# Second cross attention of a two-layer transformer kernel: where in a slot TensorE turns the probabilities

## The chip, the cores and the metric

The kernel runs on one core of a Trainium2 chip. A core has TensorE (PE, matrix products; PEld is its loading of weights), VectorE (DVE), ScalarE (ACT), GpSimd (POOL) and SyncE (SP, which here only issues transfers). The engines run side by side, each through its own list of instructions in order, and wait for each other by semaphores. TensorE has two clock levels, 1.2 and 2.4 GHz; the profile gives the granted clock as a share of the full one. The metric is the device time of one execution in microseconds (us), less is better.

## The reference

Two layers stand one after the other on x (4 x 1024 rows of 256). Each is self attention, cross attention on a context of 77 rows, and a gated feed-forward. The change touches the cross attention of the second layer alone (16 heads of 64):

```python
h = layer_norm(hidden_states, norm2_g, norm2_b)
q = (h @ wq).reshape(b, n, H, HD).transpose(0, 2, 1, 3)       # H, HD = 16, 64
k = (kv_in @ wk).reshape(b, l, H, HD).transpose(0, 2, 1, 3)   # l = 77
v = (kv_in @ wv).reshape(b, l, H, HD).transpose(0, 2, 1, 3)
probs = jax.nn.softmax(einsum('bhnd,bhld->bhnl', q, k) * HD ** -0.5, axis=-1)
out = einsum('bhnl,bhld->bhnd', probs, v).transpose(0, 2, 1, 3).reshape(b, n, H * HD)
hidden_states = out @ wo + bo + hidden_states
```

## The kernel before

The stage is the function `cross_block` (L2597), here with `narrow` false. The 4096 rows are cut into eight tiles of 512, and the 16 heads into eight pairs. One tile and one pair make a **slot**; there are 64 slots, n = 8t + p. For a slot p stands for its place in the tile, 0 to 7. The keys and values of the context were made in an earlier stage. Float32 precision is held by splitting each operand into a high and a low part and adding three products (hi x hi, lo x hi, hi x lo).

Every engine runs the same loop over n with its own part of the work, and parts of different slots stand in the body of one n. TensorE's body in the kernel before is, in this order:

- `score(n)` (L2998 on): 24 matmuls of 64 rows against 78 columns into the score bank `s` (matmuls on L3020). It waits until DVE has emptied `s`.
- `query(n + 2)` (L2986 on, matmuls on L2994): six matmuls, the query of the slot after next. None for n of 62 and more.
- `values(n - 3)` (L3037 on, L3046): two float32 matmuls, which the trace shows as four. It waits for `t_done`: ScalarE's copy of the turned probabilities of slot n - 3.
- `project(...)` (L3050 on, L3062): 24 matmuls of the output projection, in the slots with p = 7, 0, 3 and 4 only.
- `flip(n - 2)` (L3024 on, L3034): eight transposes of the probabilities into the one turned bank `t`. It waits for `t_done`, here that ScalarE has copied the bank of slot n - 3 out, and for `p_norm`, that GpSimd has divided the probabilities of slot n - 2 by their sums.
- `turn(...)` (L2977 on, L2983): eight transposes of normalised rows for a tile to come, in the slot with p = 5 of the first six tiles.

ScalarE's body in slot n is the exponential of slot n (L2951), the high part of the query (`f_q_hi`, L2931), the high part of the output of slot n - 3 (`f_o_hi`, L2938), in the slot with p = 6 of the first six tiles four instructions that scale the turned rows (`f_ht` L2915, `f_h_hi` L2920), and last the copy of the turned bank of slot n - 2 (`f_probs_t`, L2966). ScalarE can't do one of them ahead of the one listed before it.

DVE's body is the maximum of the scores (`f_mx`, L2878), their difference (L2882), sums and reciprocals of the slot before (as the loop numbers them), in slots behind a project the addition to x, the low parts of query (`f_q_lo`, L2851) and output (`f_o_lo`, L2857), in the slot with p = 1 of the first six tiles the statistics of rows (L557 to L569), and normalised rows in p = 4. GpSimd divides (L2812).

Query, output, projection and turned rows share four banks `r0` to `r3`, handed out in the order of the program; `clear(u)` waits until the fourth unit back has been emptied. The change leaves this order of units as it was.

Of the kernel before, what the change touches and what calls it, by code (L numbers as in the profile page):

```python
# [96 lines left out]
class Program:  # L97
# [2499 lines left out]
    def cross_block(self, L, x_sb, ident, g, b, wq, wo, bo):  # L2597
# [5 lines left out]
        SLOTS = TILES * PAIRS  # L2603
# [17 lines left out]
        def q_of(n):  # L2621
            if narrow:
                t = (n - 1) // PAIRS + 1
                return [(t, c) for c in range(QCH)] if n % PAIRS == 1 and 0 < t < TILES else []
            return [divmod(n + 2, PAIRS)] if 0 <= n < SLOTS - 2 else []

        def acc_of(n):
            if not 0 <= n < SLOTS:
                return None
            if narrow:  # L2630
                return (n // PAIRS, n % PAIRS // 2) if n % 2 else None
            return divmod(n, PAIRS)

        def y_of(n):
            for part, first in ((0, 7), (1, 11)):
                t, j = divmod(n - first, PAIRS)
                if 0 <= t < TILES and j < 2:
                    return (t, part, j)
            return None

        def turn_of(n):
            t, p = divmod(n - TURN_AT, PAIRS)
            return t + LEAD if p == 0 and 0 < t + LEAD < TILES else None
# [19 lines left out]
        with ExitStack() as st:  # L2663
# [305 lines left out]
            def _(pe):  # L2969
# [7 lines left out]
                def turn(t):  # L2977
                    pe.wait_ge(n_["chain"], (t + 1) * self.STATS_STEPS)
                    for c in range(DC):
                        u = at["tp", t, c]  # L2980
                        clear(u)
                        for j in range(TB):
                            ins = t_.transpose(bank[u % 4][:, j * P:(j + 1) * P], xhat[:, j, c * P:(c + 1) * P], ident[:, :])  # L2983
                        ins.then_inc(r_ready, 1)

                def query(t, c):  # L2986
                    u = at["q", t, c]
                    pe.wait_ge(hh_done, DC * (t + 1))
                    if not narrow:
                        pe.wait_ge(hl_done, t + 1)  # L2990
                    clear(u)
                    passes = [(k, 0, 0) for k in range(DC)] if narrow else self.H_PASSES
                    for j, (k, a, bb) in enumerate(passes):
                        ins = t_.matmul(bank[u % 4][:, :], wqr[a][:, k, c * P:(c + 1) * P], h[bb][t % 2][:, k, :],  # L2994
                                        start=j == 0, stop=j == len(passes) - 1)
                    ins.then_inc(r_ready, 1)

                def score(n):  # L2998
                    t, p = divmod(n, PAIRS)
                    bt = t // 2  # L3000
                    if p == 0 and t % 2 == 0:
                        pe.wait_ge(kv_in[bt % KVB], KV * (bt // KVB + 1))
                    if n > 0:
                        pe.wait_ge(s_free, n)
                    if narrow:
                        if p == 0:
                            pe.wait_ge(moved, 96 * (t + 1))
                        passes = [(qs[t % 2], p, kt[bt % KVB][0])]
                        rows = 3 * HD
                    else:  # L3010
                        pe.wait_ge(q_lo, n + 1)
                        q0, q1 = qn
                        k0, k1 = kt[bt % KVB]
                        passes = [(q0, n % 4, k0), (q0, n % 4, k1), (q1, n % 4, k0)]
                        rows = HD
                    for qb in range(TB):
                        for x, (q, slot, k) in enumerate(passes):
                            for r in range(2):
                                part = slice(64 * r, 64 * r + rows)
                                ins = t_.matmul(sbk[:, r, qb * MP:(qb + 1) * MP], q[part, slot, qb * P:(qb + 1) * P], k[part, p, :],  # L3020
                                                start=x == 0, stop=x == len(passes) - 1, tile_position=(64 * r, 0))
                    ins.then_inc(s_ready, 1)

                def flip(n):  # L3024
                    if n > 0:
                        pe.wait_ge(t_done, n)
                    if narrow:
                        busy = kt[0][0][:, :, :].rearrange("p j m -> p (j m)")
                        for r in range(2):
                            t_.matmul(tbk[:, r, :], busy[:, 0:P], busy[:, 0:512], start=True, stop=True)  # L3030
                    pe.wait_ge(p_norm, n + 1)
                    for r in range(2):
                        for qb in range(TB):
                            ins = t_.transpose(tbk[0:M, r, qb * P:(qb + 1) * P], pr[:, n % PR, r, qb, :], ident[:, :])  # L3034
                    ins.then_inc(t_ready, 1)

                def values(n):  # L3037
                    t, c = acc_of(n)
                    bt, u = t // 2, at["acc", t, c]
                    pe.wait_ge(t_done, n + 1)  # L3040
                    clear(u)
                    pairs = (n - 1, n) if narrow else (n,)
                    for x, m in enumerate(pairs):
                        for r in range(2):
                            row = W * (2 * x + r)
                            ins = t_.matmul(bank[u % 4][row:row + W, :], vs[bt % KVB][:, m % PAIRS * 2 + r, :], pt[:, m % 2, r, :],  # L3046
                                            start=True, stop=True, tile_position=(0, row))
                    ins.then_inc(r_ready, 1)

                def project(t, part, j):  # L3050
                    u, half = at["y", t, part, j], OCH // 2
                    pe.wait_ge(kind_sem["acc"], nth("acc", t, part * half + half - 1))
                    if narrow:
                        pe.wait_ge(wo_in, WOL)
                    else:
                        pe.wait_ge(w_lo, 2)
                    clear(u)
                    for k in range(2):
                        tok = slice((2 * j + k) * P, (2 * j + k + 1) * P)
                        work = [(c, x, w) for c in range(part * half, part * half + half) for x, w in (((0, 0),) if narrow else ((0, 0), (0, 1), (1, 0)))]  # L3060
                        for i, (c, x, w) in enumerate(work):
                            ins = t_.matmul(bank[u % 4][:, k * D:(k + 1) * D], o[x][:, c, tok], wor[w][:, c, :],  # L3062
                                            start=i == 0, stop=i == len(work) - 1)
                    ins.then_inc(r_ready, 1)
# [9 lines left out]
                for n in range(FIRST, LAST):  # L3074
                    if 0 <= n < SLOTS:
                        score(n)
                    for key in q_of(n):
                        query(*key)
                    if acc_of(n - 3):
                        values(n - 3)  # L3080
                    if y_of(n):
                        project(*y_of(n))
                    if 0 <= n - 2 < SLOTS:
                        flip(n - 2)
                    if turn_of(n - 1):
                        turn(turn_of(n - 1))

# [341 lines left out]
```

## Time and profile before

| | us |
|---|---|
| median of three runs | 4222.43 |
| lowest and highest of them | 4221.16 and 4227.47 |
| the profiled execution | 4226.14 |
| its span, first to last instruction | 4224.3 |
| this stage's slots in it, about | 3475.7 to 3916.2 |

In the timeline rows the first number is the start of a group of instructions in us from the span's start, the second its duration, then come engine, line, operation, output<-input by the program's names, shapes, and how many instructions the row joins; in square brackets stands the idle time of the engine ahead of it and who ended it. Matmuls are pipelined, so one starts before the one ahead has ended: what a part costs TensorE is read from start to start.

### The profile page before, as it was taken

How to read it: one execution, taken by the hardware profiler on the slowest of the kernel's cores; microseconds unless marked ns; L12 is line 12 of the kernel's file. 1: busy time of each engine (PE TensorE's matmuls, PEld its weight loads, DVE VectorE, ACT ScalarE, POOL GpSimd, SP SyncE). 2: the span in 40 equal slices, each digit the busy share in tenths (PEclk: the TensorE clock that was granted, in tenths of full speed). 3: DMA queues.
4: the chain of work that ended last, by engine and by line, in shares of the span. 5: the costliest groups of instructions: out<-in, count | busy, mean ns of one | idle time of the engine just before them, and what ended most of it. 6: DMA issues, size and time to landing. Idle time of an engine off the chain costs nothing. (4 is left out here: it accounts for less than half of the span.)

```text
span 4224.3 us, 64439 instructions
## 1 busy us (share of the span) xinstructions
PE 3916.2 (93%) x24639; PEld 2597.8 (61%) x24639; DVE 2766.8 (65%) x4547; ACT 1839.8 (44%) x2746; POOL 1859.1 (44%) x1203
## 2 busy tenths in 40 slices
PE   3799999995898997998999999999999979999899
PEld 2543443433456886885666666666666647777787
DVE  6599999953446654435767666676767637665665
ACT  1367777771453333442333333333333324444333
POOL 1288970001113102004777877877787753222200
PEclk9789999986779998997999999999999989999999
DMA  4734434405631105883211121111112010000100
GB/s 158 181 56 75 60 57 46 45 1 79 106 54 49 25 13 177 305 308 123 73 54 51 51 76 51 51 57 70 51 51 73 29 31 10 10 10 1 42 14 17
DMA packets 314325, 294.96 MB, mean 70 GB/s; under 512 B 133324, under 2 KB 237196, under 8 KB 313764
## 3 DMA queue, kind: packets, MB, share of 16 engines
q1 hardware_dynamic: 311364, 281.88, 25.8%
q0 software_dynamic: 2656, 8.97, 0.7%
q8 instruction: 197, 3.23, 0.3%
q14 instruction: 108, 0.88, 0.1%
HBM read 161.92 MB, written 127.28 MB: 68 GB/s over the span
## 5 line engine op out<-in xcount | busy, mean ns | idle before, releaser
L1741 POOL TENSOR_TENSOR f_sums<-f_sums,f_probs 128x1024 f32<-128x1024 f32 x384 | 915.5, 2384 | 154.6 <-ACT f_probs L1860 116.9
L1860 ACT ACTIVATE f_probs<-f_st 128x1024 f32<-128x1024 f32 x512 | 525.0, 1027 | 938.6 <-PE f_st L1906 933.9
L1758 DVE TENSOR_REDUCE f_mx<-f_s 128x1 f32<-128x512 f32 x1024 | 659.8, 686 | 381.0 <-PE f_s L1883 369.6
L1369 DVE TENSOR_REDUCE f_mx<-f_s 128x1 f32<-128x512 f32 x1024 | 638.7, 683 | 53.2 <-PE f_s L1501 31.2
L1481 ACT ACTIVATE f_probs<-f_st 128x512 f32<-128x512 f32 x1024 | 536.1, 600 | 234.1 <-PE f_st L1518 233.8
L1883 PE MATMUL f_s<-f_k,f_q 64*128 64x512 f32 x3072 | 514.7, 414 | 19.1 <-DMA f_k<-k 12.9
L1906 PE MATMUL f_st<-f_q,f_k 64*128 64x512 f32 x3072 | 486.0, 390 | 1.1 <-ACT f_probs L1860 1.0
L1920 PE MATMUL f_acc<-f_probs,f_v 128*64 128x512 f32 x2048 | 466.1, 597 | 0.0
L1883 PEld LDWEIGHTS f_s<-f_k,f_q 64*128 64x128 f32 x3072 | 341.4, 189 | 166.8 <-issue 112.5
L1906 PEld LDWEIGHTS f_st<-f_q,f_k 64*128 64x128 f32 x3072 | 367.0, 185 | 25.8 <-ACT f_probs L1860 3.8
L1518 PE MATMUL f_st<-f_q,f_k 50*128 50x512 f32 x1024 | 336.1, 480 | 6.6 <-ACT f_probs L1481 6.4
L588 POOL TENSOR_TENSOR f_ve<-f_var,f_const 128x4 f32<-128x4 f32 x48 | 10.0, 209 | 698.4 <-DVE f_var L569 698.2
L1518 PEld LDWEIGHTS f_st<-f_q,f_k 50*128 50x128 f32 x1024 | 137.5, 188 | 283.7 <-ACT f_probs L1481 262.6
L1920 PEld LDWEIGHTS f_acc<-f_probs,f_v 128*64 128x64 f32 x2048 | 141.5, 137 | 266.1 <-issue 257.2
L1501 PE MATMUL f_s<-f_k,f_q 48*128 48x512 f32 x1024 | 267.9, 457 | 22.8 <-DMA f_k<-k 22.5
L1530 PE MATMUL f_acc<-f_probs,f_v 128*32 128x512 f32 x2048 | 279.3, 619 | 0.0
L1781 DVE RECIPROCAL f_rd<-f_s 128x512 f32<-128x512 f32 x64 | 214.9, 3358 | 71.7 <-PE f_s L1929 71.7
L1906 PE MATMUL f_st<-f_m,f_mones 64*128 64x512 f32 x1024 | 248.4, 390 | 0.0
L3281 ACT ACTIVATE f_gate<-f_pg,f_bias 128x512 f32<-128x512 f32 x128 | 88.0, 688 | 348.8 <-PE f_pg L3327 348.8
L765 DVE TENSOR_TENSOR f_stage<-f_pc,f_stage 128x512 f32<-128x512 f32 x160 | 110.3, 691 | 190.2 <-ACT f_stage L795 190.1
L1737 POOL TENSOR_TENSOR f_sums<-f_probs 128x1024 f32<-128x1024 f32 x64 | 153.2, 2394 | 184.0 <-ACT f_probs L1860 184.0
L3206 DVE SCALAR_TENSOR_TENSOR f_u<-f_pa,f_bias,f_gate 128x512 f32<-128x512 f32 x128 | 96.1, 751 | 201.4 <-PE f_pa L3327 195.7
(320 smaller groups left out, 7861.8 us busy)
## 6 DMA issues: line engine op xcount, KB each, us to landing
q<-f_stage SPq DMA_DIRECT2D x80, 512.0 KB, 2.9
k<-f_stage SPq DMA_DIRECT2D x80, 512.0 KB, 2.8
f_q<-q SPq DMA_DIRECT2D x32, 1024.0 KB, 5.1
f_k<-k SPq DMA_DIRECT2D x32, 1024.0 KB, 7.5
v<-f_v_stage SPq DMA_DIRECT2D x64, 256.0 KB, 3.1
f_v<-v SPq DMA_DIRECT2D x32, 512.0 KB, 8.7
f_q<-q SPq DMA_DIRECT2D x96, 128.0 KB, 4.3
f_k<-k SPq DMA_DIRECT2D x96, 128.0 KB, 7.1
```

What stands on the lines that cost most here:

```text
L1369: v.tensor_reduce(mx[:, i % 2, c:c + 1], bank[u % 4][:, :], AX_X, ALU.max).then_inc(s_free, 1)
L1481: a_.activation(probs[:, n % NP, e % 2, :], stb[k % 3][:, :], ACT.Exp, scale=L.scale).then_inc(p_ready, 1)
L1501: t.matmul(bank[u % 4][:, :], q[cur][rows, j, qb * P:(qb + 1) * P], k_[cur][rows, j, f * HALF:(f + 1) * HALF], start=True, stop=True, tile ...
L1518: t.matmul(stb[n % 3][:, :], k_[cur][rows, j, c * P:(c + 1) * P], q[cur][rows, j, half * HALF:(half + 1) * HALF], start=True, stop=True, t ...
L1530: ins = t.matmul(acc[W * h:W * h + W, :], vs[cur][:, c, h, :], p, start=c == 0, stop=c == KC - 1, tile_position=(0, W * h))
L1741: g_.tensor_tensor(out, out, probs[:, n % NP, :, :], ALU.add).then_inc(sum_done, 1)
L1758: v.tensor_reduce(mx[:, i % 2, c:c + 1], bank[u % 3][:, :], AX_X, ALU.max).then_inc(s_free, 1)
L1781: v.reciprocal(rd[:, half, :], bank[u % 3][:, :]).then_inc(s_free, 1)
L1860: a_.activation(probs[:, s % NP, :, :], stb[s % 2][:, :, :], ACT.Exp, scale=L.scale).then_inc(p_ready, 1)
L1883: ins = t.matmul(bank[u % 3][:, :], q[cur][rows, a, qb * P:(qb + 1) * P], k_[cur][rows, c, f * HALF:(f + 1) * HALF], start=r == 0, stop=r ...
L1906: ins = t.matmul(stb[s % 2][:, h, :], lhs, rhs, start=r == 0, stop=r == 3, tile_position=(64 * h, 0))
L1920: ins = t.matmul(acc[W * h:W * h + W, :], vs[cur][:, c, h, :], probs[:, s % NP, h, :], start=c == 0, stop=c == KC - 1, tile_position=(0, W ...
```

## The change

TensorE's call of `flip(n - 2)` moves from behind `project` to directly behind `score(n)`, ahead of `query`, `values` and `project`. No instruction is added or removed, and the lists of the other four engines are the same.

```diff
                 for n in range(FIRST, LAST):
                     if 0 <= n < SLOTS:
                         score(n)
+                    if 0 <= n - 2 < SLOTS:
+                        flip(n - 2)
                     for key in q_of(n):
                         query(*key)
                     if acc_of(n - 3):
                         values(n - 3)
                     if y_of(n):
                         project(*y_of(n))
-                    if 0 <= n - 2 < SLOTS:
-                        flip(n - 2)
                     if turn_of(n - 1):
                         turn(turn_of(n - 1))
```

TensorE in the kernel before, slot 30 (tile 3, p = 6), from the last matmuls of its scores to the first of the next slot's:

```order
L3020 MATMUL f_s<-f_k_hi,f_q_lo 128x78 x2
L2994 MATMUL f_r<-f_h_hi,f_wq_hi 128x512
L2994 MATMUL f_r<-f_h_lo,f_wq_hi 128x512
L2994 MATMUL f_r<-f_h_hi,f_wq_lo 128x512
L2994 MATMUL f_r<-f_h_hi,f_wq_hi 128x512
L2994 MATMUL f_r<-f_h_lo,f_wq_hi 128x512
L2994 MATMUL f_r<-f_h_hi,f_wq_lo 128x512
L3046 MATMUL f_r<-f_probs_t,f_v 64x512 x2
L3034 MATMUL f_t<-ident,f_probs 77x128 x8
L3020 MATMUL f_s<-f_k_hi,f_q_hi 128x78 x2
```

The eight transposes (L3034) stand last, with the values (L3046) ahead of them. The same stretch of TensorE in the changed kernel:

```order
L3020 MATMUL f_s<-f_k_hi,f_q_lo 128x78 x2
L3034 MATMUL f_t<-ident,f_probs 77x128 x8
L2994 MATMUL f_r<-f_h_hi,f_wq_hi 128x512
L2994 MATMUL f_r<-f_h_lo,f_wq_hi 128x512
L2994 MATMUL f_r<-f_h_hi,f_wq_lo 128x512
L2994 MATMUL f_r<-f_h_hi,f_wq_hi 128x512
L2994 MATMUL f_r<-f_h_lo,f_wq_hi 128x512
L2994 MATMUL f_r<-f_h_hi,f_wq_lo 128x512
L3046 MATMUL f_r<-f_probs_t,f_v 64x512 x2
L3020 MATMUL f_s<-f_k_hi,f_q_hi 128x78 x2
```

The transposes moved ahead of the query and the values; between the values and the next transposes only the next scores are left.

ScalarE in the same slot 30, word for word the same in both kernels:

```order
L2951 ACTIVATE f_probs<-f_probs 128x616
L2931 ACTIVATE f_q_hi<-f_r 128x512
L2938 ACTIVATE f_o_hi<-f_r 128x512
L2915 ACTIVATE f_ht<-f_r,f_b,f_g 128x512 x2
L2920 ACTIVATE f_h_hi<-f_r,f_b,f_g 128x512 x2
L2966 ACTIVATE f_probs_t<-f_t 77x1024
L2951 ACTIVATE f_probs<-f_probs 128x616
```

Nothing moved here: the copy of the turned bank (L2966) still stands behind the output's high part (L2938), which reads what the values wrote.

## Rows read from the trace of the kernel before

**Rows 1.** The page's first line: span and instructions.
```profile
span 4224.3 us, 64439 instructions
```
**Rows 2.** Stretches: length, busy PE, PEld, DVE, ACT, POOL, clock, DMA share, GB/s.
```profile
3490.00:3900.00 410.00, 404.05 (x3329) 306.57 (x3330) 277.83 (x487) 183.64 (x271) 114.19 (x116) 0.99 0.04 8
3475.00:3493.00 18.00, 17.77 (x97) 14.40 (x96) 10.89 (x23) 6.04 (x10) 1.22 (x1) 0.50 0.00 1
3514.00:3517.00 3.00, 3.00 (x8) 1.72 (x9) 2.56 (x5) 1.37 (x3) 2.46 (x2) 0.50 0.00 0
```
**Rows 3.** Waits of 3490 to 3900: who for whom, us in total, times, longest.
```profile
POOL f_probs L2812 <- DVE f_rden L2890: 290.9, 62, 7.3
```
**Rows 4.** Timeline of TensorE, slot 25 (p = 1) and the start of slot 26.
```profile
3641.89 0.30 PE L3020 MATMUL f_s<-f_k_hi,f_q_hi 64*128 64x78 f32 x2
...
3643.35 0.50 PE L2994 MATMUL f_r<-f_h_hi,f_wq_hi 128*128 128x512 f32 x1
...
3644.94 1.08 PE L3046 MATMUL f_r<-f_probs_t,f_v 77*64 77x512 f32 x4
3645.95 1.10 PE L3034 MATMUL f_t<-ident,f_probs 128*77 128x128 f32 x8
3646.98 0.30 PE L3020 MATMUL f_s<-f_k_hi,f_q_hi 64*128 64x78 f32 x2
```
**Rows 5.** Timeline of ScalarE, slot 30 (p = 6), and one row of slot 31.
```profile
3678.23 0.59 ACT L2938 ACTIVATE f_o_hi<-f_r 128x512 fp32r<-128x512 f32 x1
3678.71 1.45 ACT L2915 ACTIVATE f_ht<-f_r,f_b,f_g 128x512 f32<-128x512 f32 x2
...
3681.36 1.03 ACT L2966 ACTIVATE f_probs_t<-f_t 77x1024 f32<-77x1024 f32 x1
...
3683.66 0.60 ACT L2938 ACTIVATE f_o_hi<-f_r 128x512 fp32r<-128x512 f32 x1 [0.19 <-PE f_r L3046]
```
**Rows 6.** Timeline of TensorE, slot 31 (p = 7).
```profile
3678.99 0.30 PE L3020 MATMUL f_s<-f_k_hi,f_q_hi 64*128 64x78 f32 x2
...
3680.97 0.47 PE L2994 MATMUL f_r<-f_h_hi,f_wq_hi 128*128 128x512 f32 x1 [0.46 <-ACT f_h_hi L2920]
...
3682.54 1.08 PE L3046 MATMUL f_r<-f_probs_t,f_v 77*64 77x512 f32 x4
```
**Rows 7.** Timeline of TensorE and ScalarE in the last slots, 63 and 64.
```profile
3890.82 1.08 PE L3046 MATMUL f_r<-f_probs_t,f_v 77*64 77x512 f32 x4 [0.37 <-ACT f_probs_t L2966]
...
3894.77 1.03 PE L3034 MATMUL f_t<-ident,f_probs 128*77 128x128 f32 x8
...
3895.84 1.02 ACT L2966 ACTIVATE f_probs_t<-f_t 77x1024 f32<-77x1024 f32 x1 [2.47 <-PE f_t L3034]
...
3896.91 1.08 PE L3046 MATMUL f_r<-f_probs_t,f_v 77*64 77x512 f32 x4 [1.11 <-ACT f_probs_t L2966]
```
**Rows 8.** Timeline of VectorE: slots 25 and 26, and the low output of slot 31.
```profile
3647.11 0.68 DVE L2857 TENSOR_TENSOR f_o_lo<-f_r,f_o_hi 128x512 fp32r<-128x512 f32 x1
...
3649.84 0.79 DVE L2878 TENSOR_REDUCE f_mx<-f_s 128x8 f32<-128x616 f32 x1
...
3684.30 0.69 DVE L2857 TENSOR_TENSOR f_o_lo<-f_r,f_o_hi 128x512 fp32r<-128x512 f32 x1
```
**Rows 9.** Timeline of ScalarE, slot 26 (p = 2).
```profile
3651.50 0.72 ACT L2951 ACTIVATE f_probs<-f_probs 128x616 f32<-128x616 f32 x1 [3.40 <-DVE f_probs L2882]
...
3653.08 1.02 ACT L2966 ACTIVATE f_probs_t<-f_t 77x1024 f32<-77x1024 f32 x1
```
**Rows 10.** Timeline of TensorE, slots 5 and 6 of the first tile.
```profile
3510.10 1.09 PE L2983 MATMUL f_r<-ident,f_xhat 128*128 128x128 f32 x8 [0.88 <-DVE f_xhat L2836]
...
3513.70 0.70 PE L2994 MATMUL f_r<-f_h_hi,f_wq_hi 128*128 128x512 f32 x1 [0.52 <-DVE f_q_lo L2851]
...
3516.46 1.42 PE L3046 MATMUL f_r<-f_probs_t,f_v 77*64 77x512 f32 x4
...
3517.80 1.10 PE L3034 MATMUL f_t<-ident,f_probs 128*77 128x128 f32 x8
```

## The prediction

> **What bounds the kernel now.** The change acts in one stage of the span [rows 1], so I read that stage first by stretches: in the 410 us from 3490 to 3900 TensorE is busy for 404.05, DVE for 277.83, ScalarE for 183.64, and the granted clock is 0.99 of the upper level, 2.4 GHz [rows 2]. TensorE bounds the stage, and each us in which it waits is a us of the kernel. The timeline of one slot gives the price of each part, from start to start [rows 4]: scores 1.46 us, query 1.59, values 1.01, flip 1.03, together 5.09. All parts follow each other without a wait. A project adds 2.94: in the last slots the flip starts 3.95 behind the values, whose own 1.01 goes off [rows 7].
>
> So the question is whether the flip finds its inputs ready at its new place. It has two. GpSimd's division is far ahead: GpSimd itself waited 290.9 us of the 410 for work, 4.7 a slot [rows 3], and the flip of a slot comes two slots behind its scores; moving it up by 2.60 us (query and values) leaves this input in time. The other is the copy of slot n - 3 by ScalarE, which must have emptied the bank. That one is the heart.
>
> **The chain behind the wait.** ScalarE does the copy behind the high part of the output, and that reads what TensorE's values wrote in the same slot. This order stands in both kernels. Let V be the start of the values in a slot. The output's high part starts 1.12 behind V when it has to wait for the values (3682.54 to 3683.66) [rows 5, 6]. What follows it starts 0.48 later (3678.23 to 3678.71) [rows 5]. The copy lasts 1.02, and TensorE goes on 0.05 behind its end (3895.84 + 1.02 = 3896.86, then 3896.91) [rows 7]. So the next flip can start at V + 1.12 + 0.48 + 1.02 + 0.05 = **V + 2.67**. Where does TensorE want it? Before: query of the next slot and its values stood between, so V + 1.01 + 1.03 + 1.46 + 1.59 + 1.01 = V + 6.10, and nothing waited. Now: values 1.01, scores 1.46, and then the flip, at **V + 2.47**. Query and values of the next slot are queued behind it.
>
> **The sum, place by place.**
>
> (a) Plain slots. The wait is 2.67 - 2.47 = 0.20. It falls only where no project and no turn stands between the values and the next flip, since a project covers 2.94 and a turn, eight transposes like the flip, about 1.03. Projects are in p = 7, 0, 3, 4, so the flips of p = 0, 1, 4, 5 are covered; p = 6 is covered by the turn of p = 5 in the first six tiles. What is left: p = 2 in seven tiles (in the first there is no copy yet), p = 3, 6 and 7 in tiles 6 and 7 only, which is 13 flips with p = 3 elsewhere counted in (b). 13 x 0.20 = **+2.6 us**.
>
> (b) p = 3 in tiles 1 to 5. In p = 1 DVE runs the statistics behind the low part of the output. That low part starts 0.64 behind the high part (3683.66 to 3684.30) [rows 5, 8], so at V + 1.12 + 0.64 = V + 1.76, V in p = 1; before, it came 0.6 us sooner in the slot. The maximum of p = 2 starts 2.73 behind it (3647.11 to 3649.84) [rows 8], at V + 4.49; the exponential 1.66 behind that (3649.84 to 3651.50) [rows 8, 9], the copy 1.58 behind the exponential (3651.50 to 3653.08) [rows 9]: V + 7.73, and it frees TensorE at V + 8.80. TensorE wants the flip of p = 3 at V + 1.01 + 1.46 + 0.20 + 1.03 + 1.59 + 1.01 + 1.46 = V + 7.76. Wait 1.04, five times: **+5.2 us**.
>
> (c) p = 7 in the first six tiles. In p = 6 ScalarE runs four scalings between output and copy; the copy starts 2.65 behind them (3678.71 to 3681.36) [rows 5]. The flip of p = 7 is free at V + 1.12 + 0.48 + 2.65 + 1.03 + 0.05 = V + 5.33 instead of the wanted V + 2.47: wait 2.86. Before, the query of p = 7 already waited for the same scalings: 3680.97 - 3678.99 - 1.46 = 0.52 [rows 6]. That one ends before the new one does, and goes. Net 2.34, six times: **+14.0 us**.
>
> (d) The end. With no scores left, the values of slots 60 to 63 waited for the copy of their own probabilities: 0.43 once (the row's bracket has 0.37) and 1.11 three times [rows 7], 3.8 in all. With the flip ahead, projects cover three of these copies, and only the last is bare: the values of 62 stand behind the flip of 63 and its copy behind their output, V + 2.67 against V + 1.01, 1.66. Net **-2.1 us**.
>
> (e) The clock. In the first tile TensorE waited three times within 4 us (0.88 and 0.52 in the rows shown), and then ran at 0.50, which is 1.2 GHz, from 3514 to 3517 [rows 2, 10]. There query and values cost 4.10 us (3513.70 to 3517.80) instead of 1.59 + 1.01 = 2.60: 1.5 us. A wait of 2.86 with transposes behind it, as in (c), is nearest to this row, so I take one such fall for each: 6 x 1.5 = **+9.0 us**. Bounds: nothing, since TensorE waited 1.11 twice near the end, with 6 us between, and its clock held; and twice as much, if the fall lasts through a second such stretch.
>
> (f) The beginning. From 3475 to 3493 the clock stands at 0.50 though TensorE is busy [rows 2]; it rises behind that, in slot 2. Now the first flip comes ahead of the query of slot 2. If the rise comes later by one stretch like the 3 us at 0.50 in (e), that is half of it, **+1.5 us**; bounds 0 and +5.
>
> (g) The new neighbours (values to scores, scores to flip, flip to query). No row shows them. The nearest is the change from scores to query, where the last pair of scores takes about 0.1 us more than those inside. I take 0, as one such neighbour goes for each that comes, with 0.1 x 64 = 6.4 us to either side.
>
> Sum: 2.6 + 5.2 + 14.0 - 2.1 + 9.0 + 1.5 = **+30.2 us**. On the profiled execution's 4226.1 that is 4256.3; the median of the runs is 3.7 lower, so I predict 4252.6, say **4253 us**.
>
> **Rivals.** *The clock holds* (e and f at 0): +19.7, 4242. For it speaks that it held at 1.11 twice; against it, that the new wait is two and a half times as long. *The clock falls for longer*, also at the start: +9 to +18 more, 4262 to 4271. *The waits are absorbed.* For it: TensorE's weight loading is busy only 306.57 of 410 us, 75% [rows 2], so it might catch up. Then only (d) is left, about 4220, within 0.2%. Against it: scores, query, values and flip start in fixed steps, and a step that starts late has no shorter form behind it. The Trainium skill (Perfetto Trace Analysis, Identifying the Most-Contended Engine) says that matmul busy time is no good measure of how near TensorE is to its limit and that weight loading is to be read instead; by it the stage would have a quarter of its time free, and this rival would be the forecast. No run here shows yet which holds; the fixed steps in the trace speak against it. *Faster.* If the copy of the bank were done by V + 2.47, no flip would wait. Then the 0.52 of (c) is gone six times (3.1), the end gives 3.8 less 1.7, and if (g) falls well, 6.4: 11.6 less, 4211. It turns on 0.20 us in the plain slots, but on 2.86 in (c), where the four scalings can't move; so it is nearly shut. That the change does nothing is ruled out by the order of the instructions.
>
> **How the numbers follow.** Forecast with falls of the clock 0.50; clock holds 0.25; clock falls longer 0.10; absorbed 0.11; faster 0.04. The likeliest has its own range of 4246 to 4260 with (g). The range for 8 in 10 takes in the clock that holds, with (g) at its low end, 4242 - 6.4 = 4236, and about half of the longer falls, 4268. A measurement tells about 0.2%, 8.4 us, from no change. Faster by more 0.04, within it 0.11, slower 0.85.
>
> **What would show it.** In the waits of the changed kernel TensorE's flip (L3034) should wait for ScalarE's copy (L2966): about 25 to 27 us in all, the longest near 2.9 in p = 7 of the first six tiles, near 1.0 in p = 3 of tiles 1 to 5, and 0.2 elsewhere. The query's wait for `f_h_hi` should be gone, and of the waits of the values for copies one near 1.7 be left. The granted clock should dip behind each wait of (c). DVE, ScalarE and GpSimd keep their busy time. The prediction is wrong if the flips wait but the stage isn't longer (absorbed), if the flips in p = 7 wait under 2 us (chain misread), or if slots without any wait have another length than 5.09 (neighbours).

## The result and the profile after

The changed kernel took 4252.97 us, median of five runs (4246.03 to 4258.73), against 4221.16 us, median of five runs of the kernel before (4217.26 to 4227.47). The ratio is 1.0075, 95% interval 1.0063 to 1.0088: 0.75% slower. The prediction was 4253, range 4236 to 4268.

That the sum meets the median to the last digit is luck in part: the term for the plain slots was 4.9 us too high, the terms for p = 3 and for the first tile together 4.6 us too low, and one statement of the prediction was false. So the profile is read term by term below.

The page's first line, as [rows 1]:

```profile
span 4251.2 us, 64439 instructions
```

The stage again runs on TensorE, and now it waits. The stretch that answers to the first of [rows 2], same columns:

```profile
3490.00:3900.00 410.00, 381.55 (x3068) 292.20 (x3068) 261.09 (x449) 176.68 (x255) 104.62 (x110) 0.95 0.04 8
```

TensorE's busy time in the 410 us fell from 404.05 to 381.55, and the mean clock from 0.99 to 0.95. From the first score to the last project the stage took 462.8 us (3471.49 to 3934.30) instead of 433.0 (3475.69 to 3908.72): **+29.8 us**. The rest of the span was 2.9 us shorter in this execution; nothing in it was changed.

Who makes TensorE wait, in the waits of the stage (3475 to 3945; who for whom, us in total, times, longest):

```profile
PEld f_t L3034 <- ACT f_probs_t L2966: 31.4, 28, 2.9
...
PE f_t L3034 <- ACT f_probs_t L2966: 25.8, 13, 2.8
...
PE f_t L3034 <- POOL f_probs L2812: 0.3, 1, 0.3
```

The flips wait for ScalarE's copy, in all 25.8 us, the longest 2.8. These are the 13 waits that the timeline marks: six of 2.81 in p = 7, five of 1.09 in p = 3 of tiles 1 to 5, and in tile 0 one of 2.41 and one of 1.09. The waits of 0.2 of the plain slots aren't in this total; they are read from the starts of the flips. The query's wait for `f_h_hi` is gone from the list. The timeline of tile 1 between p = 6 and p = 7 shows the chain link by link, the counterpart of [rows 5, 6] (TensorE and ScalarE, in order of time):

```profile
3576.91 1.08 PE L3046 MATMUL f_r<-f_probs_t,f_v 77*64 77x512 f32 x4
...
3577.92 0.31 PE L3020 MATMUL f_s<-f_k_hi,f_q_hi 64*128 64x78 f32 x2
...
3578.04 0.60 ACT L2938 ACTIVATE f_o_hi<-f_r 128x512 fp32r<-128x512 f32 x1 [0.42 <-PE f_r L3046]
...
3578.53 1.44 ACT L2915 ACTIVATE f_ht<-f_r,f_b,f_g 128x512 f32<-128x512 f32 x2
...
3581.18 1.03 ACT L2966 ACTIVATE f_probs_t<-f_t 77x1024 f32<-77x1024 f32 x1
...
3582.26 1.99 PE L3034 MATMUL f_t<-ident,f_probs 128*77 128x128 f32 x8 [2.81 <-ACT f_probs_t L2966]
```

The rows belong to slots 14 and 15. With V = 3576.91 the flip starts at V + 5.35, and the scores stand 1.46 wide from V + 1.01, so it was wanted at V + 2.47: 2.88 later, of which the row marks 2.81 as idle time. Here is also the clock: this flip's eight transposes take 1.64 us to the next query instead of 0.86, and the 3 us from its start on stand at half clock:

```profile
3582.00:3585.00 3.00, 2.74 (x11) 2.55 (x12) 0.07 (x1) 0.81 (x2) 1.22 (x1) 0.50 0.00 0
```

A plain slot, counterpart of [rows 4], slot 14 (p = 6), where no flip waits. It takes 4.90 us instead of 5.09: the flip costs 0.86 (3574.48 to 3575.34) ahead of the query, where it cost 1.03 ahead of the scores.

```profile
3573.02 0.30 PE L3020 MATMUL f_s<-f_k_hi,f_q_hi 64*128 64x78 f32 x2
3574.48 1.10 PE L3034 MATMUL f_t<-ident,f_probs 128*77 128x128 f32 x8
3575.34 0.48 PE L2994 MATMUL f_r<-f_h_hi,f_wq_hi 128*128 128x512 f32 x1
3576.91 1.08 PE L3046 MATMUL f_r<-f_probs_t,f_v 77*64 77x512 f32 x4
3577.92 0.31 PE L3020 MATMUL f_s<-f_k_hi,f_q_hi 64*128 64x78 f32 x2
```

And p = 3 in tile 3 (slot 27), counterpart of [rows 8, 9]. DVE's low output and the maximum behind the statistics, GpSimd's division, ScalarE's copy, and TensorE's flip:

```profile
3661.30 0.69 DVE L2857 TENSOR_TENSOR f_o_lo<-f_r,f_o_hi 128x512 fp32r<-128x512 f32 x1 [0.33 <-ACT f_o_hi L2938]
...
3664.04 0.79 DVE L2878 TENSOR_REDUCE f_mx<-f_s 128x8 f32<-128x616 f32 x1
...
3666.68 1.22 POOL L2812 TENSOR_TENSOR f_probs<-f_probs,f_rden 128x616 f32<-128x616 f32 x1 [5.58 <-DVE f_rden L2890]
...
3667.27 1.01 ACT L2966 ACTIVATE f_probs_t<-f_t 77x1024 f32<-77x1024 f32 x1
...
3668.34 1.10 PE L3034 MATMUL f_t<-ident,f_probs 128*77 128x128 f32 x8 [1.09 <-ACT f_probs_t L2966]
```

The copy ends at 3668.28 and lets the flip go. But GpSimd's division ends at 3667.90, only 0.38 earlier, while the flip was wanted at 3667.18 (its scores start at 3665.72 and are 1.46 wide). The prediction had called this input far ahead.

### The profile page after: what moved, and what is told of

It reads as the page before. It is cut to its first block and busy times, and to the rows that moved or that the text cites. A ratio compares the mean times of both kernels' runs of the same rounds, so it can differ in the third digit from the quotient of the medians.

```text
span 4251.2 us, 64439 instructions
## 1 busy us (share of the span) xinstructions
PE 3918.8 (92%) x24639; PEld 2604.7 (61%) x24639; DVE 2773.8 (65%) x4547; ACT 1844.6 (43%) x2746; POOL 1858.8 (44%) x1203
## 5 line engine op out<-in xcount | busy, mean ns | idle before, releaser
L1883 PE MATMUL f_s<-f_k,f_q 64*128 64x512 f32 x3072 | 515.4, 414 | 18.4 <-DMA f_k<-k 12.2
L1501 PE MATMUL f_s<-f_k,f_q 48*128 48x512 f32 x1024 | 268.1, 457 | 19.8 <-DMA f_k<-k 19.5
```

The source lines that it names most:

```text
L1501: t.matmul(bank[u % 4][:, :], q[cur][rows, j, qb * P:(qb + 1) * P], k_[cur][rows, j, f * HALF:(f + 1) * HALF], start=True, stop=True, tile ...
L1883: ins = t.matmul(bank[u % 3][:, :], q[cur][rows, a, qb * P:(qb + 1) * P], k_[cur][rows, c, f * HALF:(f + 1) * HALF], start=r == 0, stop=r ...
```

## Experiments

Slot lengths from one start of scores to the next, in us, each from the one profiled execution of its kernel, for tiles 1 to 5. The last column is the stage, from the start of the first scores to the start of the last project. The ratios below are against runs of the kernel before made together with each set of experiments (medians 4219.6 to 4220.4).

| kernel | p = 1 | p = 2 | p = 3 | p = 7 | last scores to last project | stage |
|---|---|---|---|---|---|---|
| before | 5.09 | 5.09 | 7.87 to 7.97 | 8.38 to 8.47 | 19.79 | 433.0 |
| changed | 4.90 | 5.17 | 9.01 to 9.09, once 10.52 | 12.10 to 12.36 | 17.88 | 462.8 |
| copy first | 4.90 | 5.16 | 8.76, once 10.26 | 8.46 | 19.58 | 438.3 |
| flip behind query | 4.93 | 5.16 | 7.88 to 7.96 | 9.3 to 9.4, or 10.6 | 17.78 | 437.3 |
| extra matmuls | 4.90 | 5.15 | 9.10 or 10.6 | 7.93 (p = 6: 7.85) | 17.77 | 457.1 |
| copy ahead of scaling | 4.90 | 5.16 | 10.5 to 10.6 | 10.8 to 10.9 | 17.87 | 458.1 |
| statistics in p = 0 | 4.90 | 5.11 | 8.06 | 13.3 to 13.4 | 17.87 | 460.7 |
| copy first and statistics | 4.90 | 4.90 | 7.85 to 7.93 | 8.38 to 8.47 | 16.39 | 424.7 |
| early where covered | 4.90 | 5.16 | 7.88 | 9.34, 10.7 or 13.6 | 18.81 | 446.1 |
| early in p = 7 only | 5.09 | 5.09 | 7.88 to 7.97 | 11.1 to 11.4, once 12.64 | 19.62 | 452.9 |
| statistics alone | 5.09 | 5.09 | 7.88 | 8.39 to 8.47 | 19.61 | 432.2 |

The whole kernel scatters by 10 to 37 us between executions, of the kernel before too (4206.61 to 4236.95 in one set), so a ratio tells a few tenths of a per cent, and the slots tell the mechanism: where the clock doesn't fall they repeat to 0.1 us from tile to tile. A stage length is of one execution, and how often the clock falls in others wasn't seen.

### Copy first

```diff
 (ScalarE, slot n)
+                    (copy of the turned bank of slot n - 2)
                     if 0 <= n < SLOTS:
                         act.wait_ge(s_free, n + 1)
                         a_.activation(flat, flat, ACT.Exp, ...)
...
-                    (copy of the turned bank of slot n - 2)
```

> The changed order on TensorE, and ScalarE's copy of the turned bank moved from the end of its slot to its front, ahead of the exponential. If the changed kernel is slower because the copy stands behind the output's high part (and the scaling) on ScalarE, all waits of the flips for the copy go: plain slots 4.90 us, p = 7 back to about 8.3 (its query then waits some 0.4 for the scaling), the last values wait under 0.3; the whole 9 us below the kernel before, near 4212. If it is slower because query and values stand later in their slot (late low parts of query and output on VectorE), nothing of that changes and it stays near 4250.

4221.0 us, ratio 1.0006 (0.9991 to 1.0021). With the flip in its new place and only the copy moved, the 0.75% are gone. All waits for the copy went, and p = 7 is back at 8.46. So nearly all of the price is where the prediction put it: the copy's place on ScalarE's list. In p = 7 the late query and values are no price. But the expected gain of 9 us didn't come, and in the profiled execution the stage is still 5.3 us longer than before. Waits of the stage (3475 to 3935) and two rows of slot 27:

```profile
PE f_t L3034 <- POOL f_probs L2812: 5.6, 8, 0.8
...
PE f_r L2994 <- ACT f_h_hi L2920: 1.8, 6, 0.3
```

```profile
3655.96 1.22 POOL L2812 TENSOR_TENSOR f_probs<-f_probs,f_rden 128x616 f32<-128x616 f32 x1 [5.59 <-DVE f_rden L2890]
...
3657.32 1.07 PE L3034 MATMUL f_t<-ident,f_probs 128*77 128x128 f32 x8 [0.79 <-POOL f_probs L2812]
```

The second input shows behind the first: in p = 3 the flip now waits 0.79 us for GpSimd's division, which ends at 3657.18, and the scores 0.19 for DVE. The slot keeps 0.88 of its 1.2 us, and in one of the five tiles the clock fell behind this wait of 0.79 (p = 3 at 10.26). The scores' wait for DVE is also why p = 2 stays at 5.16 here in tiles 1 to 5, while it is 4.91 and 4.90 in tiles 6 and 7, which have no statistics.

### Flip behind the query

```diff
                         score(n)
-                    if 0 <= n - 2 < SLOTS:
-                        flip(n - 2)
                     for key in q_of(n):
                         query(*key)
+                    if 0 <= n - 2 < SLOTS:
+                        flip(n - 2)
```

> Flip between query and values. If the price is the 2.67 us from values to the emptied bank, plain slots and p = 3 are free of waits, since the query's 1.6 us lies between, and p = 7 keeps a wait of about 0.75: some 4 us for it and 2 us less at the end, 4217 to 4226, no measurable difference from the kernel before, and no fall of the clock in p = 7. If any flip ahead of the values costs, it comes out well above 4230.

4225.1 us, ratio 1.0009 (0.9998 to 1.0021). The time is in the expected range, its make-up isn't as expected. In p = 7 the flip doesn't wait; the query ahead of it waits for the scaling, 1.3 us and not 0.5, since no flip stands any more between the values of p = 6 and the query. Waits of the stage:

```profile
PE f_r L2994 <- ACT f_h_hi L2920: 8.0, 6, 1.3
```

After this wait of 1.3 us the clock held in three of six tiles (p = 7 at 9.3 to 9.4) and fell in three (10.6), which was not expected.

### Extra matmuls against the fall of the clock

```diff
 (score(n), ahead of its matmuls)
+                    if turn_of(n - 3) and n > 0:
+                        fill = kt[bt % KVB][0][:, :, :].rearrange("p j m -> p (j m)")
+                        for k in range(12):
+                            t_.matmul(sbk[:, k % 2, :], fill[:, 0:P], fill[:, 0:512], start=True, stop=True)
```

> The changed kernel with twelve extra matmuls (128 x 512, some 2.6 us) ahead of the scores in p = 7 of the first six tiles; the scores overwrite what they write. They end within the 2.8 us that the flip waits anyway. If the 1.2 GHz stretch behind that wait costs, it goes and the kernel is about 6 x 1.3 = 8 us faster than the changed one, near 4244, with p = 7 slots of about 10.9 us instead of 12.2. If the clock plays no part, p = 7 stays at 12.2 or grows.

4249.2 us, ratio 1.0069 (1.0050 to 1.0088), so by the whole nothing can be told from the changed kernel. By the slots it can. The extra matmuls take 2.94 us in the length of p = 6, and p = 7 is 7.93; together 15.8 against 17.0 to 17.3 in the changed kernel, 1.2 to 1.5 less, with more work done. In the timeline (slots 14 and 15) the flip follows the scores without a wait and takes 0.86 us, that is at full clock:

```profile
3572.96 3.01 PE L3019 MATMUL f_s<-f_k_hi 128*128 128x512 f32 x12
3575.90 0.30 PE L3024 MATMUL f_s<-f_k_hi,f_q_hi 64*128 64x78 f32 x2
...
3577.36 1.10 PE L3038 MATMUL f_t<-ident,f_probs 128*77 128x128 f32 x8
...
3578.22 0.48 PE L2994 MATMUL f_r<-f_h_hi,f_wq_hi 128*128 128x512 f32 x1
```

So the fall is real and costs 1.2 to 1.5 us each time in tiles 1 to 5. The stage is 5.7 us shorter and not 8, mainly because the clock now fell in p = 3 of three tiles (10.6 instead of 9.1), where it had fallen once.

### The copy ahead of the scaling

```diff
 (ScalarE, slot n)
-                    if turn_of(n - 2):
-                        scale(turn_of(n - 2))
                     (copy of the turned bank of slot n - 2)
+                    if turn_of(n - 2):
+                        scale(turn_of(n - 2))
```

> The changed kernel with the four scalings of p = 6 behind the copy instead of ahead of it. The flip of p = 7 should wait 0.2 instead of 2.8, its query then 1.2 for the scaling, and the clock should hold there: p = 7 at about 9.2 us instead of 12.2, six times, 18 us less than the changed kernel, near 4235. Waits of p = 2 and p = 3 stay. If p = 7 is long for another reason, it stays at 12.

4237.6 us, ratio 1.0039 (1.0023 to 1.0055); half of the loss is back in the median. That is near the expected 4235, but not by the expected way: p = 7 came to 10.85 and not 9.2 in tiles 1 to 5, and the stage of the profiled execution, the slowest of the six, is only 4.7 us shorter than in the changed kernel. Why the median is 15 us lower isn't shown. The wait of the flip is gone and the query's for the scaling is there as expected, but the clock falls behind that one too, and behind the 1.09 in p = 3 in all five tiles. Both in the timeline, of tile 2 and of tile 3:

```profile
3634.18 0.62 PE L2994 MATMUL f_r<-f_h_hi,f_wq_hi 128*128 128x512 f32 x1 [0.99 <-ACT f_h_hi L2920]
...
3661.93 1.99 PE L3034 MATMUL f_t<-ident,f_probs 128*77 128x128 f32 x8 [1.09 <-ACT f_probs_t L2964]
```

The same wait of 1.09 with transposes of 1.99 us here, and of 1.10 us in slot 27 of the changed kernel: a wait of this size alone doesn't settle whether the clock falls.

### Statistics in p = 0

```diff
 (VectorE, slot n; the loops start one slot earlier)
-                    if turn_of(n + 3):
-                        self.norm_stats(dve, n_, x_sb, turn_of(n + 3))
+                    if turn_of(n + 4):
+                        self.norm_stats(dve, n_, x_sb, turn_of(n + 4))
```

> The changed kernel with VectorE's statistics in the slots with p = 0 instead of p = 1. If they make p = 3 long (9.1 us against 7.9 before), p = 3 of tiles 1 to 5 comes to about 8.05, like tiles 6 and 7 where there are none, and the stage is about 5 us shorter, 6.5 if the fall of the clock in tile 1 goes too: near 4247. If something else holds the flip of p = 3, it stays at 9.1.

4243.9 us, ratio 1.0054 (1.0027 to 1.0081). p = 3 came to 8.06 in tiles 1 to 5, as expected: the statistics made some 1.0 of the 1.2 us there. The stage is only 2.1 us shorter, since in p = 7 of tiles 1 to 5 the clock now stays at 1.2 GHz for about 6.8 us instead of 3.4 (13.4 instead of 12.2). The stretches of 1 us show 0.50 from 3687 to 3693 in tile 3, where the changed kernel has 3698 to 3701.

### Copy first and statistics in p = 0 together

The diffs of copy first and of the statistics, both applied to the changed kernel.

> Both repairs together: ScalarE's copy at the front of its slot and VectorE's statistics in p = 0. With the copy first alone, the flip of p = 3 still waited 0.79 us for GpSimd's division and the scores 0.2 for VectorE. If both come from the statistics, no wait is left in p = 3 (7.85 us) and p = 2 (4.90), and tiles 1 to 5 take 0.6 us less each than in the kernel before: stage near 430 us against 433.0, total near 4217. If GpSimd is late for another reason, p = 3 stays at 8.7.

4215.8 us, ratio 0.9991 (0.9976 to 1.0006): by the whole, no difference from the kernel before. Stage 424.7. No flip of the tiles behind the first waits for the copy, and one 0.6 us for GpSimd (3540 to 3920):

```profile
PE f_r L2994 <- ACT f_h_hi L2920: 1.5, 5, 0.3
...
PE f_t L3034 <- POOL f_probs L2812: 0.6, 1, 0.6
```

The same kernel, run again:

> The kernel with both repairs once more, with more rounds: its stage took 424.7 us against 433.0 in the kernel before, 8.3 less, 0.2% of the whole. If that is a gain of the kernel and not of one execution, the stage is 423 to 427 again and the ratio stays below 1, about 0.998; if the one execution was lucky, the stage comes out near 430 and the ratio at 1.

4215.4 us, ratio **0.9976 (0.9955 to 0.9996)**, stage 424.2. Of the two sets only this one puts the whole kernel's gain over the kernel before clear of nothing, and barely. The stage is shorter by 8.3 and 8.8 us, with the same slots in tiles 1 to 7 to 0.1 us; against the changed kernel the version is 38 us of stage shorter. Its counterpart is the kernel before with the diff of the statistics alone, the flip in its old place:

> The kernel before with VectorE's statistics in p = 0 and nothing else: the flip in its old place. If the gain of the repaired kernel comes from the early flip (0.2 us less in p = 1, 2 and 6, and a shorter end), this one shows none of it: all slots of tiles 1 to 7 as in the kernel before, 5.09 in p = 1, 2 and 6, stage 432 to 434. If the statistics alone bring it, its stage is as short as 425.

4223.1 us, ratio 1.0012 (0.9994 to 1.0031), stage 432.2, and slots as in the kernel before. So the statistics alone bring no gain: it comes with the early flip once nothing holds it, 0.19 us each in p = 1, 2 and 6, and with a shorter end (16.39 instead of 19.61). What of the end is due to the flip and what to the copy's new place wasn't separated; the kernel before with the copy first wasn't run.

### Early only where something covers it

```diff
+                    early = n % PAIRS in (0, 1, 4, 5) or (n % PAIRS == 6 and turn_of(n - 2)) or n >= SLOTS
+                    if early and 0 <= n - 2 < SLOTS:
+                        flip(n - 2)
...
+                    if not early and 0 <= n - 2 < SLOTS:
+                        flip(n - 2)
```

> The flip early only where a project or a turn stands ahead of it (p = 0, 1, 4, 5, and 6 of the first six tiles) and at the end; late as before in the others. By the chain from values to the emptied bank no flip waits: p = 1 and 6 at 4.90, p = 2 at 5.09, p = 3 at 7.9, p = 7 at 8.45, the end 1.9 us shorter, no dips of the clock in tiles 1 to 7: stage 428 to 430 us, total near 4217. If an early flip costs whatever stands ahead of it, it is slower than before.

4238.7 us, ratio 1.0043 (1.0024 to 1.0063): a miss. Behind tile 0 the flips do nearly as the chain says: from 3540 to 3920 one of them waits, 1.1 us, at the end. But p = 7 is 9.34, 10.7 or 13.6 instead of 8.45. With the flip of p = 6 moved ahead, its 1.03 us no longer stand between the values and the next query, and that waits for the scaling:

```profile
PE f_r L2994 <- ACT f_h_hi L2920: 6.7, 5, 1.3
```

Five waits of 1.3 us: behind one no fall of the clock (9.34), behind two a short one (10.7), and behind two one of some 10 us (13.6; the stretches of 1 us show 0.50 from 3631 to 3640). (p = 2 came to 5.16 and not 5.09.) The late flip had been the cover of another wait.

### Early in p = 7 only

```diff
+                    early = n % PAIRS == 7 and turn_of(n - 3)
```

> The flip early only in p = 7 of the first six tiles. The values of p = 6 then have the late flip behind them, so the early one is wanted at V + 3.50 and free at V + 5.33: wait 1.83, less the 0.5 that the query no longer waits, 1.3 us each, and 2.8 where the clock falls: 8 to 17 us in all, 4230 to 4239. Other slots as in the kernel before. If the wait in p = 7 isn't the copy behind the scalings, p = 7 stays near 8.4.

4240.1 us, ratio 1.0043 (1.0023 to 1.0063). In tiles 1 to 5 five waits of 1.9 us, as expected, p = 7 at 11.1 to 11.4 (once 12.64), the other slots as before. The stage is 19.8 us longer, of the 29.8 of the whole change: some 2.8 us for each such slot, the upper end of what was expected, and 4.2 in tiles 0 and 5 with a longer fall of 6.8 us, which was not; the whole came out 1 us above the expected range.

```profile
PE f_t L3034 <- ACT f_probs_t L2966: 9.6, 5, 1.9
```

## Why the prediction was right, and where not

| term | predicted | measured in the stage |
|---|---|---|
| (a) plain slots and (g) neighbours | +2.6, and 0 | -2.3 |
| (b) p = 3, tiles 1 to 5 | +5.2 | +7.3 |
| (c) and (e) p = 7, tiles 1 to 5 | 5 x 3.84 = +19.2 | +18.9 |
| tile 0: rest of (c) and (e), and (f) | +5.3 | +7.8 |
| (d) the end | -2.1 | -1.9 |
| sum | +30.2 | +29.8 |

**The bound and the chain** held. TensorE's waits became time. V + 2.67 and V + 5.33 were met to 0.02 us, and the first experiment took the copy off the chain and with it the whole loss of the median. The rival in which the waits are absorbed is out: weight loading was busy for only 292.20 of 410 us, and yet TensorE made up nothing. That the listed waits came to 25.8, inside the forecast 25 to 27, is part luck: 3.5 us of them are the two in tile 0 that nobody forecast, and the forecast 2.6 of the plain slots isn't in them.

**(c)** 2.88 measured against 2.86. **(e)** was the boldest term, taken from one row of the kernel before. The clock fell around all six waits, and the extra matmuls gave 1.2 to 1.5 us back for each in tiles 1 to 5, 1.5 predicted; in tile 0 the fall lasted twice as long. **(d)** was met: the last bare copy cost 1.60 us, 1.66 predicted.

**(a) and (g)** failed in sign. The waits of 0.2 are there: the flip of p = 2 in tile 3 starts at V + 2.68, 0.22 late, and p = 2 takes 5.17, and 4.90 with all repairs. But the step "one such neighbour goes for each that comes", with 0 for the neighbours, was wrong: a slot without a wait is 4.90 and not 5.09. That is the third sign that the prediction itself had named for being wrong. The flip costs 0.17 less ahead of the query than ahead of the scores. In slots with a project the gain is hardly there, 7.83 to 7.93 against 7.87 to 7.97. The bound of 6.4 us held it. The values of p = 1, the scores and the flip of p = 2 in tile 3:

```profile
3659.55 1.08 PE L3046 MATMUL f_r<-f_probs_t,f_v 77*64 77x512 f32 x4
3660.55 0.30 PE L3020 MATMUL f_s<-f_k_hi,f_q_hi 64*128 64x78 f32 x2
...
3662.23 1.10 PE L3034 MATMUL f_t<-ident,f_probs 128*77 128x128 f32 x8
```

**(b)** was low by 1.5 for a fall of the clock in tile 1 and by 0.1 for each wait (four slots longer by 1.12 to 1.21). Worse is the step under it, "this input in time": GpSimd's division of a slot comes in the body of the next slot, not in its own, and behind the statistics it is 0.8 us late for the new place, as copy first showed. Its 290.9 us of idle time [rows 3] say how much time it had, not when its work came. It didn't spoil the sum only because the copy was later still by 0.4 us.

**Tile 0** was undersized, and **(f)** had the wrong mechanism: the clock didn't rise later. Slot 3 took 9.41 us instead of 5.09: its flip waited 2.41 us for the copy of slot 0, which stands behind the split of the output weights (1.9 us on ScalarE) and the query's high part. The clock stood at 1.2 GHz from 3489.5, before this wait was over and behind one of 1.20 that the scores of slot 3 had for DVE.

```profile
3491.93 1.99 PE L3034 MATMUL f_t<-ident,f_probs 128*77 128x128 f32 x8 [2.41 <-ACT f_probs_t L2966]
```

The chain of (a), written for settled tiles, was never walked through the first slots. Slot 2, on the other hand, was 1.6 us shorter because the clock rose at 3482.7, ahead of the first moved instruction (3484.29); that is no doing of the change. Nor is all of slot 3: in the kernel that is early in p = 7 only, where nothing has moved so far, slot 2 took 5.14 and slot 3 6.63, with a fall of its own behind a wait of 1.15. Slots 2 and 3 together took 11.8 us there and in the kernel before, and 14.6 in the changed one, so the change cost 2.7 in them. The rest of tile 0's 7.8 is 4.8 in p = 7, where the clock stood at 1.2 GHz for 6.8 us (3.84 predicted), and 0.4 in p = 6.

## What to carry to other kernels

When an instruction is moved ahead on one engine, walk the lists of the others: what empties its buffer may stand behind the very work that it has overtaken, and then both lists have to be changed together. Here the flip alone cost 0.75%, and flip, copy and statistics together gained 0.09% in one set (interval -0.06 to 0.24%) and 0.24% in another (0.04 to 0.45%). Where a step is moved away, ask also which wait it covered; and idle time of an engine says nothing of when its result arrives, so follow each input to the loop body in which it is made.

## What the runs showed of the hardware

Around each wait of 2.8 us (twelve, in the changed kernel and the one with the statistics moved) and of 1.9 us (five, early in p = 7 only) TensorE's clock fell to 1.2 GHz, and around waits of 0.8 to 1.3 us in some tiles and not in others of the same kernel. A fall lasted about 3.4 us in p = 7 of the changed kernel's tiles 1 to 5, about 6.8 us there in the kernel with the statistics moved, with the same wait ahead of it, and about 10 us twice in the kernel that is early where covered. What decides whether it falls, and for how long, wasn't settled here. It cost 1.2 to 1.5 us for the shorter fall.

The same eight transposes cost TensorE 0.86 us with the query behind them and 1.03 with the scores behind them, both at full clock, read from start to start. The rows of weight loading show where they differ: the first load for the scores starts 0.16 us behind the last of the transposes, the first for the query directly behind it. Why was not tried.
